# Mixture-of-experts stage by tiles of 128 slots: which operand is stationary, how rows are loaded, and 71 tiles in blocks of four, two and one instead of 78 in blocks of four and two

## What is computed

```python
x = x + attention(layernorm(x))            # 16 heads of 32, causal, latent keys and values of 128
n = layernorm(x).reshape(4096, 512)
probs = softmax(n @ gate_w.T)              # 8 experts
w, ids = top_k(probs, 2); w = w / sum(w)   # each token goes to two experts
for e in range(8):                         # F = 352
    down[e] = (silu(n @ w_gate[e]) * (n @ w_up[e])) @ w_down[e]
out = x + sum_e gates[:, e] * down[e] + shared_ffn(n)
```

## Time and profile before

| | us |
|---|---|
| median of 3 runs | 2332.29 (2331.23 to 2332.98) |
| the profiled execution, its own time | 2336.36 |
| its span, first to last instruction | 2334.6 |
| first matmul of the expert stage | 1803.4 |
| last matmul of the expert stage starts | 2329.0 |

### The profile page before, as it was taken

How to read it: one execution, slowest core, us unless ns; L and a number is a source line. 1 busy time by engine, 2 the same in 40 slices (tenths; PEclk the granted TensorE clock), 3 DMA queues, 4 the chain that set the end, 5 groups by cost and what they waited for, 6 DMA issues and landing times. The chain is left out here.

```text
span 2334.6 us, 32228 instructions
## 1 busy us (share of the span) xinstructions
PE 2192.8 (94%) x11695; PEld 1377.6 (59%) x11695; DVE 1480.2 (63%) x3296; ACT 1027.3 (44%) x1925; POOL 1165.0 (50%) x730
## 2 busy tenths in 40 slices
PE   6999999999999999999999997899997999999999
PEld 5777544444444444444444432677775788888887
DVE  4665886767766676676776742667565455556554
ACT  3333255555655555555555555131222343434433
POOL 1010166556665565655666557364644445544544
PEclk9999699999999999999999988899998999999999
DMA  5678702313123141151412111434433756666662
GB/s 167 246 256 268 171 24 51 77 37 91 37 55 74 38 91 37 46 142 38 91 37 55 53 30 44 127 121 134 137 105 119 240 184 222 197 215 208 207 212 87
DMA packets 168254, 278.66 MB, mean 119 GB/s; under 512 B 28571, under 2 KB 71067, under 8 KB 168096
## 3 DMA queue, kind: packets, MB, share of 16 engines
q1 hardware_dynamic: 145152, 210.43, 31.0%
q0 software_dynamic: 22944, 66.19, 9.1%
HBM read 191.25 MB, written 88.71 MB: 120 GB/s over the span
## 5 line engine op out<-in xcount | busy, mean ns | idle before, releaser
L928 ACT ACTIVATE b_pt<-b_st 128x512 f32<-128x512 f32 (+3 forms) x1280 | 612.5, 535 | 478.6 <-DVE b_st L890 192.0
L749 POOL TENSOR_TENSOR b_acc<-b_acc,b_pt 128x1024 f32<-128x1024 f32 (+1 forms) x256 | 593.0, 2346 | 215.8 <-ACT b_pt L928 215.2
L868 DVE TENSOR_REDUCE b_mpart<-b_mx 128x1 f32<-128x512 f32 x768 | 512.2, 686 | 186.9 <-PE b_mx L985 184.5
L1008 PE MATMUL b_st<-b_q,b_k 97*128 97x512 f32 (+2 forms) x1280 | 499.1, 403 | 57.1 <-ACT b_pt L928 53.7
L985 PE MATMUL b_mx<-b_k,b_q 96*128 96x512 f32 (+2 forms) x1280 | 510.9, 414 | 6.7 <-DVE b_mpart L868 3.3
L985 PEld LDWEIGHTS b_mx<-b_k,b_q 96*128 96x128 f32 x1280 | 249.5, 196 | 264.3 <-DVE b_mpart L868 149.7
L1008 PEld LDWEIGHTS b_st<-b_q,b_k 97*128 97x128 f32 x1280 | 243.4, 192 | 264.9 <-ACT b_pt L928 239.7
L1021 PE MATMUL b_ob<-b_pt,b_v 128*32 128x512 f32 (+3 forms) x2560 | 305.5, 549 | 1.1 <-ACT b_pt L928 1.1
L865 DVE CUSTOM_DVE_ANT_0 b_unread<-b_mx,b_later 128x384 bf16<-128x384 f32 (+3 forms) x512 | 244.6, 484 | 91.0 <-PE b_mx L985 90.5
L749 POOL TENSOR_TENSOR b_acc<-b_pt 128x1024 f32<-128x1024 f32 x48 | 113.4, 2379 | 269.5 <-ACT b_pt L928 269.5
L1774 POOL DMA_INDIRECT e_rows<-out_dram,entry x78 | 92.8, 1190 | 128.9 <-DMA out_dram<-e_rows,entry 111.9
(11 more groups left out here) (251 smaller groups left out, 3692.9 us busy)
## 6 DMA issues: line engine op xcount, KB each, us to landing
b_q<-scr_qh SPq DMA_DIRECT2D x64, 256.0 KB, 4.6
b_k<-scr_kh SPq DMA_DIRECT2D x64, 256.0 KB, 4.0
sw_raw<-in_L_ffn_w_gate_dram SPq DMA_DIRECT2D x12, 704.0 KB, 4.5
sw_raw<-in_L_ffn_w_up_dram SPq DMA_DIRECT2D x12, 704.0 KB, 6.9
a_xin<-in_L_attn_x_dram POOLq DMA_DIRECT2D x8, 1024.0 KB, 5.8
scr_qh<-wo SPq DMA_DIRECT2D x8, 1024.0 KB, 5.0
scr_ql<-oin SPq DMA_DIRECT2D x8, 1024.0 KB, 7.2
scr_kh<-sw_raw SPq DMA_DIRECT2D x8, 1024.0 KB, 4.3
```

The source lines that it names most:

```text
L749: g.tensor_tensor(out[:, :, lo:], so_far[:, :, lo:], pt[n % NPB][:, :, lo:], ALU.add).then_inc(s_add, 1)
L868: v.tensor_reduce(part, mxb[i % NMX][:, 0:w], AX.X, ALU.max).then_inc(s_red, 1)
L928: act.activation(pt[n % NPB][:, j, lo:], stb[:, (2 * n + j) % NST, lo:], ACT.Exp, scale=SCALE).then_inc(s_exp, 1)
L1008: pe.matmul(stb[:, (2 * n + j) % NST, lo:], kb[:, h, at:at + P], qb[:, h, q * CH + lo:(q + 1) * CH], start=True, stop=True).then_inc(s_st, 1)
```

## The change

- **PE's operands.** The gate and up products now have the *rows* stationary (128 slots) and the weights moving (352 columns): 12 matmuls each a tile, into one bank each (`e_gb`, `e_ub`), with the slots on the partitions. So ACT's silu and DVE's product are one instruction of 352 columns a tile, and PE must transpose the hidden values (`turn_hidden`: three more transposes a tile, into the second of the two banks `e_tb`) before they are split and `down` uses them. Everything goes tile by tile. `down` of tile i-1 stands behind the gate and up products of tile i and ahead of `turn_hidden` of tile i.
- **Tiles.** 71 tiles in 27 blocks: twelve of four, eight of two, seven of one, in the order 4, 1, 4, 2, 4, 1, ..., 4, 2, 2, 2, 1. Each block still has a fetch of an expert's weights (2112 KB). `map_blocks` has some 26 more small instructions on DVE, and its wide ones are 648 elements instead of 368.
- **Rows.** x rows are gathered tile by tile, five tiles ahead, into eight buffers. `sums_after` says behind which tile's work the sum into `out` is made: at the earliest one tile behind its own, and the first of a block at least two behind the last of the block before. Down products have four banks.
- **Weights.** The split of block b's weights is spread by `parts_at`: gate part in the middle of the last tile of block b-2 (`early`: between the split of the x rows and that of the hidden values), up part at its end, down parts at the end of the next tile.
- **SP** fetches the weights of blocks 1 and 2, then the entries of 24 blocks, and only then block 3's weights.

```diff
-NB = WHOLES + HALVES
 TPB = SLOTS // P
-TILES = [2 if b >= 4 and b % 3 == 1 else 4 for b in range(NB)]
+UNITS = (2 * T + E * (P - 1)) // P
+TWOS, ONES = E, E - 1
+FOURS = (UNITS - 2 * TWOS - ONES) // TPB
+NB = FOURS + TWOS + ONES
+TILES = [n for i in range(FOURS) for n in (TPB, 1 + i % 2)] + [2, 2, 1]
+KINDS = (TPB, 2, 1)
 ABOVE = [sum(TILES[:b]) for b in range(NB + 1)]
-SPOT = [TILES[:b].count(TPB) if TILES[b] == TPB else WHOLES + TILES[:b].count(TPB // 2) for b in range(NB)]
+PLACE = [(b, t) for b in range(NB) for t in range(TILES[b])]
+SPOT = [sum((FOURS, TWOS, ONES)[:KINDS.index(n)]) + TILES[:b].count(n) for b, n in enumerate(TILES)]
+RING = 2 * TPB
+UNDER_WAY = 6
 PLACES = E * T + NB * SLOTS
-RUN = 87
+RUN = 91
...
+def sums_after():
+
+
+    after, at = [[] for _ in range(UNITS + 3)], 0
+    for i, (b, t) in enumerate(PLACE):
+        at = max(i + 1, at + (2 if t == 0 else 0))
+        after[at].append(i)
+    return after
...
+        def parts_at(i, late):
+
+
+            out = []
+            for b in range(1, NB):
+                free = last_tile(b - 2) if b > 1 else 2
+                if not late and i == free:
+                    out.append((b, 0))
+                if late and i == free + 1:
+                    out += [(b, 2), (b, 3)]
+                if late and i == free:
+                    out.append((b, 1))
+            return out
...
+                    for j in (0, 1, 3):
+                        sp.wait_ge(*passed(s_wl, j, b - 2))
+                    fetch_expert(nc, sp, keep, w, b, wt[b % 2], s_w[b % 2])
+                    if b == 2:
+                        for later in range(3, NB):
+                            fetch_entries(nc, sp, keep, scratch, later, s_ent)
...
+                for now in range(UNITS + 3):
+                    for i in AFTER[now]:
+                        scatter(i)
+                    if now + UNDER_WAY - 1 < UNITS:
+                        x_rows(now + UNDER_WAY - 1)
+                    for i in AFTER[now]:
+                        b = PLACE[i][0]
+                        if i == last_tile(b) and b + 1 < NB:
+                            g.wait_ge(s_sc, ABOVE[b + 1] * 16)
+                            out_rows(b + 1)
...
+                for i in range(UNITS):
+                    act.wait_ge(s_g, i + 1)
+                    act.activation(sg[:], gb[:, 0:F], ACT.Silu).then_inc(s_sg, 1)
+                    if i + 1 < UNITS:
+                        act.wait_ge(s_t, i + 2)
+                        act.activation(begun.row_high(i + 1), begun.turned(), ACT.Copy).then_inc(s_xh, 1)
+                    split(parts_at(i, False))
+                    act.wait_ge(s_ht, i + 1)
+                    act.activation(hh[:].rearrange("p f t -> p (f t)"), hb[:, 0:NF * P], ACT.Copy).then_inc(s_hh, 1)
+                    split(parts_at(i, True))
...
+                for i in range(UNITS):
+                    if i + 1 < UNITS:
+                        v.wait_ge(s_xh, i + 2)
+                        v.tensor_tensor(begun.row_low(i + 1), begun.turned(), f32(begun.row_high(i + 1)), ALU.subtract).then_inc(s_xl, 1)
+                    v.wait_ge(s_sg, i + 1)
+                    v.wait_ge(s_u, i + 1)
+                    v.tensor_tensor(hf[:], sg[:], ub[:, 0:F], ALU.mult).then_inc(s_h, 1)
+                    split(parts_at(i, False))
+                    v.wait_ge(s_hh, i + 1)
+                    v.tensor_tensor(hl[:].rearrange("p f t -> p (f t)"), hb[:, 0:NF * P], f32(hh[:]).rearrange("p f t -> p (f t)"),
+                                    ALU.subtract).then_inc(s_hl, 1)
+                    for done in AFTER[i]:
+                        add_out(done)
+                    split(parts_at(i, True))
...
+                    if i >= 4:
+                        pe.wait_ge(s_y, i - 3)
+                    down(nc, db[i % 4][:], wt[b % 2], hh, hl, 0).then_inc(s_dn, 1)
+
+                for i in range(UNITS):
+                    pe.wait_ge(s_xl, i + 1)
+                    hidden(gb, i, 0).then_inc(s_g, 1)
+                    if i + 1 < UNITS:
+                        pe.wait_ge(s_x[(i + 1) % UNDER_WAY], turns(i + 1, UNDER_WAY))
+                        turn_row(pe, begun, keep, i + 1).then_inc(s_t, 1)
+                    hidden(ub, i, 1).then_inc(s_u, 1)
+                    if i:
+                        down_row(i - 1)
+                    turn_hidden(i)
+                down_row(UNITS - 1)
```

More of the change, by code:

```diff
@@ L1860, in _ @@
+                sp.wait_ge(s_sc, UNITS * 16)
             @block.gpsimd
             def _(g):
[L1862 to L1867 removed]
@@ L1908, in step, with split @@
-                def step(b, n, first, last):
-                    for f in range(NF):
-                        hidden(b, f, first)
-                        if not last:
-                            if f:
-                                x_high(b + 1, 1 - n, range(2 * f - 2, 2 * f))
-                            split(b + 1, 1 - n, slice(f, f + 1 if f < 2 else WP))
-                over_blocks(step)
+                def split(some):
+                    for b, j in some:
+                        n = b % 2
+                        act.wait_ge(s_w[n], (b // 2 + 1) * 64)
+                        if b > 1:
+                            act.wait_ge((s_g, s_u, s_dn, s_dn)[j], ABOVE[b - 1])
+                        raw, hi, lo = parts(n)[j]
+                        act.activation(hi, raw, ACT.Copy).then_inc(s_wh[min(j, 2)], 1)
@@ L1952, in _ @@
+                for now in range(UNITS, UNITS + 3):
+                    for done in AFTER[now]:
+                        add_out(done)
             @block.tensor
             def _(pe):
[L1954 to L1960 removed]
```

332 lines of the change are left out of this document (156 added, 176 removed).

## The result

The changed kernel takes 2313.15 us, the median of four runs (2309.82 to 2320.17); the kernel before, run beside it, 2332.64 (2331.23 to 2332.98). The ratio is 0.9922 with a 95% interval of 0.9895 to 0.9948: faster by some 19 us. The profiled execution is the slowest of the four: 2320.17, span 2318.4.

A forecast was written before the change was run, and what follows sets the result against it. PE alone was taken to set the expert stage's time. Terms -45 + 4 + 1 + 16 - 1 + 8 = -17, off the median 2332.3, gave 2315 us; 8-in-10 range 2298 to 2332.

The forecast's parts named there:

- PE's work, 71 tiles: Expert stage: 71 tiles of 6.75 us instead of 78 of 6.72, with 352 columns at 0.162; -45 us.
- DVE late in single tiles, by its load: Fullest tiles of each round of eleven: sums and weight parts make DVE late by 0.1 and 0.5; +4 us.
- rows of `out`: Between blocks: scatter, landing and gather before the next block's first sum; +1 us in all, 44 at the bad end.
- third block's weights: Tiles 4 and 5: block 3's fetch behind 24 entries holds ACT, then PE, 11 us late; +16 us in all.
- PE's wait before the last down: Stage's end: PE waits 1.3 us for the low part of the last tile; part of +8 for the end.
- start of the stage: First matmul at about 1802.5 instead of 1803.4, set by weights, splits and x low part; -1 us.
- behind the last matmul: Program's end: the last one-tile block's rows come late, 11.7 us instead of 5.3; part of +8 for the end.
- phases ahead (same code): Phases before the expert stage: the prediction gave them no term.
- the rival on it: Expert stage: seven transposes a tile lower PE's clock; 2339 us at 5% of the stage; chance 0.03.
- The rival that it is hidden: Early in the stage: the wait for block 3's weights does not show, gain 33, 2299 us; chance 0.15.
- the rival's 43 us: Scatter, landing, gather between blocks bind, 1.7 us each: 2358 us; chance 0.12 slower than before, another 0.10 partial.

The follow-up runs named there:

- the second profile: The changed kernel itself run again, nothing altered, against the kernel before: 2313.56 us, ratio 0.9918.
- the kernel with splits moved: Changed kernel with block 3's splits later (first at tile 6's end), every block's up part one tile later, entries where they were: 2296.41 us, ratio 0.9879.
- The longer map: Changed kernel with DVE repeating a product and sum four times more in the map of blocks, 6.9 us: 2317.13 us, ratio 0.9968.
- with 224: The kernel with splits moved plus 11 small indirect gathers on GpSimd into a buffer nothing reads: 2299.74 us, ratio 0.9870.
- with 234: The kernel with splits moved plus 21 small indirect gathers on GpSimd into a buffer nothing reads: 2300.03 us, ratio 0.9884.

## Why the prediction came out as it did

Forecast -17, the spans differ by 16.2 and the medians by 19.5. By its own steps:

| term | forecast | profile of after |
|---|---|---|
| PE's work, 71 tiles | -45 | -47.3 |
| DVE late in single tiles, by its load | +4 | +0.5 (tile 47, cause open) |
| rows of `out` | +1 | +2.8, apart from the end |
| third block's weights | +16 | +16.2 |
| PE's wait before the last down | +1.3 | +1.5 |
| start of the stage | -1 | +3.6 |
| behind the last matmul | +6.4 | +14.1 |
| phases ahead (same code) | 0 | -7.5 |

-47.3 is what is left of 499.6 - 525.9 when the four terms under it are taken off. The total was right, and partly by luck: the two terms of the start and the end were wrong by 12 us together, and 7.5 of it came back from the phases ahead of the stage, which had been put at nothing.

- **PE's work: right.** 352 columns cost 0.160, in proportion to the 512, and a tile 6.69. The Trainium skill's rule for an isolated matmul ("TensorE: Matmul & The Clock Gate", "Back-to-back issue gap") would have 0.149, and is 0.011 short here as it was, by 0.017 and 0.010, at 512 and 256 columns. The clock stayed at 1.00 with seven transposes a tile; the rival on it is out. The start went less well: the first tile, without a down product, has 4.6 us of work and took 8.45, 3.9 lost where 1.8 was put. PE waited 1.1 for the first hidden product, and the granted clock was 0.50 in the first 3.5 us. No run took the new order of operands and the count of tiles apart; by the steps, 6.72 before and 6.69 now, the count is the gain.
- **Third block's weights: right in place, mechanism and size,** and shown by taking it away: with its splits elsewhere the step is 6.70. The rival that it is hidden is out. Within the 16 the parts differ. The wait was 11.2, forecast 11, though both its ends came over 2 us later in the stage than reckoned. The 3 us for weight parts and a sum that crowd on DVE were 0.7 of PE's waiting, and the lower clock took 4.3 instead of 1.8. In the second profile it took 2.1, which makes 14.2.
- **DVE's late products: near in number, wrong in the way.** The prediction had DVE late by its load, most of all, by 0.5, in tiles with one sum and three parts. Those (16, 27, 49) take 6.69. The seven long tiles that make 2.8 of the 3.3 us are ones in which DVE waits for rows of `out` ahead of the product: 3.0 to 3.2 us in tiles 14, 36 and 58 with two sums and no part, and 0.5 to 0.7 in tiles 20, 31, 42 and 53 with three sums and one part, more in each than the tile is late. (In tiles 14 and 58 this profile does not show the end of the wait, but the sum waits only for rows and for a down product made long before, and in the kernel with splits moved the same waits, 3.2 us each, end with the rows' landing.) In the last four the load has its share: moving one part took a third of the sum away.
- **The chain of rows binds in single tiles.** POOL still waits for scatters to land, 42.1 us (before 111.9), and 59 of 70 tile steps are 6.69, so it is far from the rival's 43 us. But it is the term that was too small, +2.8 for +1, and in the fastest kernel, with splits moved, it is all that makes tiles long. The row of the page:

```profile
L1825 POOL DMA_INDIRECT e_rows<-out_dram,entry x71 | 76.1, 1072 | 71.6 <-DMA out_dram<-e_rows,entry 42.1
```

- **Start of the stage: the step failed.** I let the start hang on weights, splits and x low on DVE, and took the four gathers off. DVE's part was nearly as reckoned (drained 37.5 behind the last `c_ex`, before 37.0). But the stage starts when all engines are drained. POOL's gathers wait for the map, through the first entries, and its drain ends 7.8 behind the last of them; what had 2.6 us of slack before is last now. The longer map shows it: 6.9 us in, 6.9 out.
- **The end: the mechanism was right, the size was not.** The last sum ends 11.7 behind the last hidden transposes, forecast 11.2. But I put 3.9 behind the sum (it was 4.4 in the kernel before), and it is 11.2: POOL's drain, which the sum had no term for.
- **What stays open:** why the drain has this length. The number of indirect transfers does not settle it: with 68 of them behind it in every kernel, the drain ahead of the stage ended 5.6 us behind the last gather in the kernel before, and 6.8 to 7.8 in the others where nothing was waited for. Open too is how much of the 19.5 us is the change's. By the pieces it is 8.6, or 11 with the second profile (stage 497.4); the comparisons with the changed kernel, or with a variant corrected by its measured pieces, give 10 to 19.5. One profile of the kernel before, with its last `c_ex` at 1766.0, cannot tell whether the phases ahead differ by chance. It lies outside the other thirteen: the attention, first to last matmul, took 1201.7 us in it and 1187.7 to 1196.9 in them. That speaks for a difference that is not chance, and no run shows where it comes from.

## What to carry to other kernels

Count tiles where PE is full: their number times the measured step was the gain, and the new way to make a tile moved its step by only 0.03. Then look at what stands in an in-order queue ahead of something that PE needs: a split four tiles early cost 16 us, and moving it was worth more than moving the fetches that made it late; small fetches of 1.1 us each are cheap only where no large one is behind them. When a product comes late, look for what its engine waited for ahead of it, before its load is blamed: here it was mostly a sum that waited for gathered rows. Where a part of a program ends for all engines at once, take the drain of each engine as a term of the path, with what precedes it.

## What the runs showed of the hardware that was not expected

- GpSimd's drain at the program's end ended 9.12 us behind its last scatter's issue in nine profiles with 213 indirect transfers for the stage (four of them issued ahead of the drain that begins it), and 9.29 in a tenth; in its last 8 us nothing moved in the DMA queues. It was 6.7 with 224, 4.2 with 234, and 2.3 in the kernel before, also with 234.
- A wait of PE for 1.79 us (tile 9, block 3's splits three tiles later) was followed by a lower granted clock and a tile of 8.2; one of 1.49 us at the same tile of the kernel with the entries left was not, the next tile took 6.68. Windows of the first and of the second:

```profile
1862.00:1868.00 6.00, 4.21 (x18) 3.69 (x17) 4.84 (x7) 1.95 (x3) 3.34 (x4) 0.77 0.80 257
1868.00:1874.00 6.00, 6.00 (x35) 5.50 (x35) 2.05 (x4) 1.11 (x3) 2.10 (x2) 0.94 1.01 360
```

```profile
1854.00:1860.00 6.00, 4.51 (x28) 3.88 (x27) 4.79 (x7) 2.37 (x5) 3.22 (x3) 1.00 0.87 313
1860.00:1866.00 6.00, 6.00 (x36) 5.56 (x35) 4.57 (x6) 2.34 (x4) 3.58 (x4) 1.00 0.60 178
```

- The time of the same code in the phases ahead of the stage moved by 15 us from profile to profile, and the stage's first tile took 7.15 to 8.46 us.
